# Q and K of both attention layers in two float32r parts, two heads in the row halves of TensorE

## What is computed

```
def attention0(x):                                   # layer 0
    q, k, v = split(x @ Wqkv)                        # 16 heads, 16 dimensions each
    scores = einsum('bhqd,bhkd->bhqk', q, k) * hd ** -0.5
    scores = where(causal, scores, -inf)
    return einsum('bhqk,bhkd->bhqd', softmax(scores), v) @ Wproj + bproj

mod = silu(cond) @ Wada + bada                       # shifts, scales and gates
x = x + gate_a * attention0(norm(x) * (1 + scale_a) + shift_a)
x = x + gate_m * (gelu((norm(x) * (1 + scale_m) + shift_m) @ W1 + b1) @ W2 + b2)

h = gamma * norm(x) + beta                           # layer 1
q, k, v = split(h @ Wqkv1.T + bqkv)
att = softmax(einsum('bhqd,bhkd->bhqk', q, k)) / sqrt(D)
h1 = einsum('bhqk,bhkd->bhqd', att, v) @ Wp.T + bp + x
return gamma * norm(h1) + beta + h1
```

## Time and profile before

| | |
|---|---|
| median of 3 runs | 1240.19 us (1234.33 to 1240.56) |
| profiled execution, its own time | 1239.17 us |
| its span, first to last instruction | 1237.4 us |
| mean granted TensorE clock | 0.986 of full speed |
| PE busy | 1164.9 us (94%) |
| DVE busy | 849.1 us (69%) |
| ACT busy | 676.6 us (55%) |
| POOL busy | 279.7 us (23%) |

### The profile page before, as it was taken

One profiled execution on the slowest core, in us unless ns is written; L12 is line 12 of the kernel. 1 busy time (PEld: TensorE's weight loads), 2 busy tenths in 40 slices (PEclk: granted clock), 3 DMA queues, 4 the chain that ended last, 5 costly groups with the idle time before them and its releaser, 6 DMA issues.

```text
span 1237.4 us, 18599 instructions
## 1 busy us (share of the span) xinstructions
PE 1164.9 (94%) x6604; PEld 591.7 (48%) x6604; DVE 849.1 (69%) x1779; ACT 676.6 (55%) x1346; POOL 279.7 (23%) x378
## 2 busy tenths in 40 slices
PE   7888999999999998999899999999989999999995
PEld 5434644464444644555345644546445553445332
DVE  4835498637886579836887379855888368764775
ACT  1173245656557465565656466565645656553673
POOL 1133032311432024301233013320233002310003
PEclk9799999999999999999999999999999999999999
DMA  4603031302432042500623024410425005200311
GB/s 166 206 2 103 3 124 33 107 14 72 111 93 65 18 113 71 139 2 18 164 44 115 2 80 104 105 54 18 118 66 139 1 2 148 55 17 32 86 33 43
DMA packets 59190, 89.35 MB, mean 72 GB/s; under 512 B 12914, under 2 KB 23762, under 8 KB 59098
## 3 DMA queue, kind: packets, MB, share of 16 engines
q1 hardware_dynamic: 58078, 87.35, 25.4%
q10 hardware_dynamic: 1020, 0.81, 0.2%
HBM read 24.41 MB, written 4.70 MB: 24 GB/s over the span
## 4 chain that ended last, share of the span: by engine, by line
PE 63%; DVE 19%; ACT 5%; SPq 5%; DMA 3%; issue 3%; POOL 1%; ACTq 0%; DVEq 0%; POOLq 0%
PE X L1037 15%; DVE MX L759 10%; PE OP L942 10%; PE X L1064 9%; PE X L1088 9%; PE SC L953 8%; PE X L972 8%; SPq L416 4%; ACT E L621 3%; DMA OC<-OE 2%; DVE STAT L768 2%; DVE XN L808 2%; DVE XR L875 1%; DVE TMP L871 1%; PE X L1052 1%
## 5 line engine op out<-in xcount | busy, mean ns | idle before, releaser
L759 DVE TENSOR_REDUCE MX<-X 128x1 f32<-128x512 f32 (+3 forms) x1024 | 533.2, 583 | 178.4 <-PE X L975 95.4
L621 ACT ACTIVATE E<-SC 128x512 f32<-128x512 f32 (+3 forms) x1024 | 459.0, 524 | 325.8 <-PE SC L953 258.6
L972 PE MATMUL X<-KS,QS 96*128 96x512 bf16 (+3 forms) x1024 | 296.5, 346 | 11.6 <-DVE MX L759 7.5
L953 PE MATMUL SC<-QS,KS 99*128 99x512 bf16 (+3 forms) x1024 | 276.1, 342 | 19.6 <-ACT E L621 12.6
L942 PE MATMUL OP<-E,V 128*32 128x512 f32 (+3 forms) x2048 | 208.2, 524 | 5.2 <-ACT OE L636 5.0
L953 PEld LDWEIGHTS SC<-QS,KS 99*128 99x128 bf16 x1024 | 93.7, 97 | 168.3 <-ACT E L621 105.9
L972 PEld LDWEIGHTS X<-KS,QS 96*128 96x128 bf16 x1024 | 97.4, 98 | 160.2 <-DVE MX L759 52.9
L541 POOL TENSOR_SCALAR_AFFINE_SELECT E<-E 128x512 f32<-128x512 f32 x128 | 87.0, 683 | 249.1 <-ACT E L621 249.1
L1088 PE MATMUL X<-XT,W 128*128 128x512 f32 x256 | 119.1, 598 | 1.2 <-ACT XT L651 1.2
L1064 PE MATMUL X<-XT,WQKV 128*128 128x512 f32 x256 | 118.2, 607 | 1.4 <-ACT XT L651 1.4
L1037 PE MATMUL X<-W,HID 128*128 128x256 f32 x512 | 115.3, 380 | 0.3 <-ACT HID L671 0.3
(11 more groups left out here) (92 smaller groups left out, 922.9 us busy)
## 6 DMA issues: line engine op xcount, KB each, us to landing
QS<-PART SPq DMA_DIRECT2D x192, 128.0 KB, 2.4
KS<-PART SPq DMA_DIRECT2D x192, 128.0 KB, 2.5
OC<-OE SPq DMA_DIRECT2D x56, 128.0 KB, 3.8
RB<-recip_sums SPq DMA_DIRECT2D x56, 128.0 KB, 2.6
XIN<-in_x SPq DMA_DIRECT2D x8, 512.0 KB, 4.9
ROW<-row_vectors SPq DMA_DIRECT2D x8, 512.0 KB, 3.7
out<-OUT SPq DMA_DIRECT2D x7, 512.0 KB, 3.2
W<-in_w SPq DMA_DIRECT2D x2, 1024.0 KB, 7.3
```

Of the source, the lines that this page charges most:

```text
L621: a.activation(E[:, at["tick"].index() % 3, j, lo:T], SC[(at["head"].index() + j) % 3][:, lo:T], ACT.Exp, scale=HD ** -0.5 if layer == 0 e ...
L759: v.reduce_max(MX[:, qt, h:h + 1], X[at["bank"].index() % BANKS][:, 0:w], AX.X, negate=True)\
L953: t_.matmul(SC[(at["head"].index() + j) % 3][:, lo:T], KS[stacks(layer, b)][0:ALL_ROWS, h, kt * P:kt * P + P], QS[stacks(layer, b)][0:ALL_ ...
L972: ins = t_.matmul(bank[:, 0:w], QS[stacks(layer, b)][0:CUT_ROWS, h, qt * P:qt * P + P], KS[stacks(layer, b)][0:CUT_ROWS, h, 0:w], start=Tr ...
```

## The change

- Q and K are cut into two float32r parts instead of three bf16 ones. ACT writes the high part, DVE the low part directly; X32 and the third cut are gone. Three products of parts matter, so a head takes 3 rows for each dimension, 48, and a spare fourth row, 64 in all. The spare rows are zero but for two that hold the maximum in two parts (in QS) and ones (in KS). Scans and scores use the same 64 rows, so the maximum's rows in QS are zeroed by a DMA before each stack.
- Even heads stand on partitions 0 to 63, odd ones on 64 to 127, so that a matmul uses 64 rows of the array (tile size 64 x 128 in the built program, where before it is 128 x 128). Scans of the two heads of a pair alternate, tile by tile.
- The mask has 128 rows and a half has 64, so it takes two matmuls (L995, L996), of 128 and 64 columns.
- SyncE issues 14 DMAs for Q and K of a layer and batch, 256 KB each but two of 64 KB, instead of 24 of 128 KB.
- Spare rows are zeroed at the start by four DMAs of 512 KB; condition tiles move into R1 and constants into RH.
- HEAD, RING and TAIL are written anew; at the start `mods` moves ahead of `turn_a`.

```diff
-CUTS = 6
-CUT_ROWS = CUTS * HD
-ALL_ROWS = CUT_ROWS + 3
-Q_PARTS = (0, 0, 0, 1, 1, 2)
-K_PARTS = (0, 1, 2, 0, 1, 0)
+CUTS = 3
+SPARE = CUTS
+ROWS_PER_DIM = CUTS + 1
+HALF_ROWS = ROWS_PER_DIM * HD
+MAX_ROWS = slice(SPARE, P, 32)
+Q_PARTS = (0, 0, 1)
+K_PARTS = (0, 1, 0)
...
 HEAD = """
-    stat_a norm_a turn_a q0 stackq0 k0 stackk0 mods rows s v0 s s s s s s s s s s s s s s s s s s s s s s s s s
...
+    stat_a norm_a mods turn_a q0 stackq0 k0 stackk0 rows v0 s s s s s s s s s s s s s s s s s s s s nm0_0 s
...
+def scan_tiles(layer):
+    return [(2 * pair + u, qt) for pair in range(PAIRS) for qt in range(TT) for u in range(2)]
+def rows_of(h):
+    return slice(HALF_ROWS * (h % 2), HALF_ROWS * (h % 2) + HALF_ROWS)
...
-            sp.wait_ge(ones_pool, 1)
+            sp.wait_ge(ones_pool, 3)
             for n in range(2):
-                sp.dma_start(KS[n][CUT_ROWS:ALL_ROWS, :, :], ONES).then_inc(ones_load, 16)
+                for stacked in (QS, KS):
+                    sp.dma_start(stacked[n][SPARE:P:ROWS_PER_DIM, :, :], SPARES).then_inc(spare_load[n], 16)
+            for n in range(2):
+                sp.wait_ge(spare_load[n], 32)
+                sp.dma_start(KS[n][MAX_ROWS, :, :], ONES).then_inc(ones_load, 16)
...
-                for part in range(3):
-                    wait(sp, (high_act, cut_low, cut_low)[part], ready[part])
+                if side == 0:
+                    sp.dma_start(QS[n][MAX_ROWS, pairs, :], ZERO[:]).then_inc(stack_dma[n][half], 16)
+                for part in range(2):
+                    wait(sp, (high_act, dense_dve)[part], ready[part] + half)
                     for r in range(CUTS):
                         if parts[r] == part:
-                            sp.dma_start((QS, KS)[side][n][r:CUT_ROWS:CUTS, heads, :],
-                                         PART[rows, side, part, :, :]).then_inc(stack_dma[n][half], 16)
+                            sp.dma_start((QS, KS)[side][n][r:P:ROWS_PER_DIM, pairs, :],
+                                         PART[:, side, part, half, :]).then_inc(stack_dma[n][half], 16)
...
-                        if t == 0:
-                            wait(dve, cut_low, at["low"].at())
                         if what[1] == "0":
-                            ins = v.tensor_tensor(X32[:, t, :], bank(t)[:], part[:, 0, t, :], ALU.subtract)
+                            ins = v.tensor_tensor(low, bank(t)[:], high, ALU.subtract)
...
-                    if what[1] == "1" or b == 0:
-                        wait(dve, dense_dve, at["by_dve"].at(1, 2))
-                        v.tensor_copy(part[:, 1], X32[:]).then_inc(cut_low, 1)
-                        wait(dve, cut_low, at["low"].at(1, 1))
-                        v.tensor_tensor(part[:, 2], X32[:], part[:, 1], ALU.subtract).then_inc(cut_low, 1)
...
-                t_.matmul(SC[(at["head"].index() + j) % 3][:, lo:T], KS[stacks(layer, b)][0:ALL_ROWS, h, kt * P:kt * P + P],
-                          QS[stacks(layer, b)][0:ALL_ROWS, h, lo:T], start=True, stop=True).then_inc(head_full, 1)
+                rows, n = rows_of(h), stacks(layer, b)
+                t_.matmul(SC[(at["head"].index() + j) % 3][:, lo:T], KSR[n][rows, h // 2, kt * P:kt * P + P],
+                          QSR[n][rows, h // 2, lo:T], start=True, stop=True).then_inc(head_full, 1)
...
-                ins = t_.matmul(bank[:, 0:w], QS[stacks(layer, b)][0:CUT_ROWS, h, qt * P:qt * P + P],
-                                KS[stacks(layer, b)][0:CUT_ROWS, h, 0:w], start=True, stop=layer == 1)
+                ins = t_.matmul(bank[:, 0:w], QSR[n][rows, h // 2, qt * P:qt * P + P],
+                                KSR[n][rows, h // 2, 0:w], start=True, stop=layer == 1)
                 if layer == 0:
-                    ins = t_.matmul(bank[:, qt * P:w], ID16[:], CAUSAL[:], start=False, stop=True)
+                    t_.matmul(bank[:, qt * P:w], IDR[rows, HALF_ROWS:3 * HALF_ROWS], CAUSAL[rows, :], start=False, stop=False)
+                    ins = t_.matmul(bank[:, qt * P + HALF_ROWS:w], IDR[rows, 0:P], CAUSAL[rows, 0:HALF_ROWS],
+                                    start=False, stop=True)
```

More of the change, by code:

```diff
@@ L216, in one_list @@
     groups = [(layer, b, s // TT) for layer, b, s in products if s % TT == TT - 1]
-    tiles = [(layer, b, n // TT, n % TT) for i in passes
+    tiles = [(layer, b, *scan_tiles(layer)[n]) for i in passes
              for layer, b, first, end in ((0, i, H * TT // 2 + EARLY, H * TT), (1, i - 1, 0, H * TT),
@@ L657, in work @@
                     for t in range(2):
[L658 removed]
+                        part, psum = PARTR[:, side, 0, t, :], bank(t)
                         if t == 0:
                             for half in range(2):
[L661 to L662 removed]
+                                wait(act, stack_dma[0][half], at["stack0"].at(STACKED))
+                                wait(act, stack_dma[1][half], at["stack1"].at(STACKED))
                         if what[1] == "0":
@@ L678, in work @@
                 elif what.startswith("max"):
-                    n, heads = int(what[3]), maxima_heads(what)
-                    rows = 3 * (heads.stop - heads.start)
+                    n, pairs = int(what[3]), maxima_pairs(what)
+                    rows = 4 * (pairs.stop - pairs.start)
                     psum = bank(0)
@@ L967, in scan @@
                 if h % (H // 2) == 0 and qt == 0:
-                    wait(pe, stack_dma[stacks(layer, b)][h // (H // 2)], 192 * (b + 1 + layer - stacks(layer, b)))
+                    wait(pe, stack_dma[stacks(layer, b)][h // (H // 2)], STACKED * (b + 1 + layer - stacks(layer, b)))
+                    if b == 0 and layer == 0:
+                        pe.wait_ge(spare_load[0], 32)
+                        pe.wait_ge(mask_load, 32)
+                    if b == 0 and layer == 1:
+                        pe.wait_ge(spare_load[1], 32)
                 claim(at["bank"].at(), scan_done, at["scan"].at(1, 1))
@@ L1111, in work @@
                 elif what.startswith("max"):
-                    wait(pe, max_pool, at["maxima"].at(4, 4))
-                    psum = bank(0).bitcast(BF16)
-                    heads = maxima_heads(what)
-                    rows = 3 * (heads.stop - heads.start)
+                    wait(pe, max_pool, at["maxima"].at(2, 2))
+                    psum = bank(0)
+                    pairs = maxima_pairs(what)
+                    rows = 4 * (pairs.stop - pairs.start)
                     for qt in range(TT):
-                        ins = t_.transpose(psum[0:rows, qt * P:qt * P + P], NMP[:, qt, 0:rows], ID16[:])
+                        ins = t_.transpose(psum[0:rows, qt * P:qt * P + P], NMP[:, qt, 0:rows].bitcast(F32), ID32[:])
                     ins.then_inc(dense_full, 1)
```

191 lines of the change are left out of this document (95 added, 96 removed).

## The result

The changed kernel takes 1298.66 us (median of 4 runs, 1295.49 to 1307.12), the kernel before 1239.89 beside it on the same chip. The ratio is 1.0496, with a 95% interval of 1.0445 to 1.0546: 59 us slower, where 49 us faster was forecast. The time lies above the range.

What follows compares the result with a forecast made beforehand. TensorE (PE) was taken as the bound. The profiled span 1237.4 - 76 (stream gain after waits) + 23 (mode changes) + 3 (start) = 1187, with 1.8 around it 1189, and median runs 1.0 higher: 1190 us, range 1115 to 1290.

Steps and rivals of the forecast that it cites:

- I take bf16's rate and full overlap between the halves: Scans and scores: 512-column matmuls at 0.108 us each, touched stream 288 us instead of 390, a change of -102.
- rival 4: Wide float32r matmuls: halves don't overlap (1349 us) or each streams like a float32 record (1375); break-even 0.17 each; chance 0.19.
- the load's 0.11: TensorE weight loads: 4-byte weights of 128 columns take some 0.11 us each, read from the small modulation matmuls.
- rival 2: Weight loads go one after another despite the halves, 0.11 us each: 1226 us, up to 1236; chance 0.13.
- The share of waits: TensorE waiting for banks that DVE and ACT free: a quarter of the 102 us gain lost, leaving -76.
- The sum of 390 us: TensorE's stream that the change touches, before it: scans, scores and masks, 390 of 1237 us.
- Layer 0's tiles: Layer 0's scans with two masks each: 0.28 us a tile, 143 us for 512 against 102 before, losing 41.
- Changes of mode: Switching TensorE's tiling: about 0.1 us each, 259 more changes, 26 us at most, taken as +23, lower end 0.
- Cutting: Dropping the third part of Q and K: 34.6 us less of DVE, counted at 0, lower end -10.
- The start: Modulation matmuls ahead of the first Q and K, and zeros through SyncE's queue: +3 us, ends 0 and +10.
- The signs I had named: Start distances, records per matmul, PE's share below 94%, DVE's near 69%, DVE's waits for PE shrinking, PE's for DVE and ACT growing.
- The last condition: Forecast wrong if time stands above 1234 us with halves overlapping: then the loss is in masks, switches or the order.

Runs made afterwards that it cites:

- new lists: The kernel before with the changed kernel's HEAD, RING and TAIL, nothing else changed: 1245.0 us, ratio 1.0043 to the kernel before.
- bf16 over all rows: The changed kernel with bf16 for stacks, parts, masks and maxima, and every scan, score and mask over all 128 rows: 1229.0 us, ratio 0.9907 to the kernel before.
- bf16 halves: The changed kernel with bf16 instead of float32r for stacks, parts, masks and maxima, row halves kept: 1229.4 us, ratio 0.9912 to the kernel before.

## Why the prediction was wrong

**The ledger.** The 59 us, from kernel to kernel: new lists +5 (1239.9 to 1245.0), lighter cutting, two parts and the second mask together, in bf16 over all rows, -16 (to 1229.0), float32r +97 (to 1325.8), halves -27 (to 1298.7). The last is some -73 of matmuls side by side and +46 of clock. Seen the other way, 44 of the 59 us are the clock's share (60 against 16) and 15 are the rest, where the forecast had -49 and no clock.

**The step that failed** is "I take bf16's rate and full overlap between the halves" for 1152 wide matmuls at 0.108 each. The rate was nearly right (one record, 0.235 us for 512 columns) and the overlap is real, but it is far from full. The table has the touched stream, from start to start in the trace, without the half of the time that it spent at the lower clock, and what the prediction had for the change, all in us:

| part | before | after | change | forecast |
|---|---|---|---|---|
| wide scans and scores, 1280 | 323 | 287 | -36 | -124 |
| narrow scores, 384 | 78 | 76 | -2 | -21 |
| layer 0's narrow scans, all masks | 98 | 127 | +29 | +41 |
| together | 499 | 490 | -9 | -102 |

Three things keep the wide ones from 0.108. First, wide matmuls follow one another 830 times, and only 271 times do two begin within 0.05 us (255 in bf16 halves); if each had a wide partner, it would be at least half of the times. Second, a pair in float32r holds PE for 0.34 us and not 0.22. With 0.17 a pair member, my own break-even of rival 4 (0.17) was reached. In bf16 the pair takes 0.23 (670.10 to 670.33), so the difference is the type's; I had the load's 0.11 in hand and counted it only for masks, and rival 2 named it only as a floor under narrow matmuls. Third, the long stretches: six wide matmuls and a product take 1.61 us where 6 x 0.108 would be 0.65, and in bf16 halves still 1.39; the stretch from 211.08 shows how, with a score that waits for a bank that ACT's exps free. How much of the missing 88 us each of the three costs, no run separates.

**What was missing altogether** is the clock. The sum went by the earlier trace rows at 0.986, and nothing in them is on half the array, so no row could tell; but 44 us more of clock's share is nearly as large as the forecast gain. I should have kept a term for it, since the earlier trace rows show the clock at 0.85 and 0.92 in the two stretches where PE is less busy.

**The other terms.** *The share of waits*: a quarter of the gain was too little. The sum of 390 us is what matmuls need; in the trace they hold PE for 505 us before (what they wait included), 524 after, 491 in bf16 over all rows and 464 in bf16 halves. The rows I read for waits were PE's own; the loads of scores waited for ACT for 105.9 us before already. ACT's exp at 0.53 us is more than twice a score, and there are three banks. *Layer 0's tiles*: 0.28 forecast, and +41 us; the clock included, the narrow scans and masks grew by just that, from 101 to 142, but 12 of it are the clock's, so the agreement is in part luck. Alone, a tile costs the scan + 0.10, then 0.06 and 0.08, so 0.40 for 384 columns; where two lie side by side, both together cost 0.42 (581.22 to 581.64 in after), below my 0.28 each:

```profile
581.22 0.45 PE L992 MATMUL X<-KS,QS 64*128 64x384 f32 x2
581.50 0.23 PE L995 MATMUL X<-CAUSAL,IDR 64*128 64x128 f32 x2
581.56 0.25 PE L996 MATMUL X<-CAUSAL,IDR 64*128 64x64 f32 x2
581.64 0.48 PE L992 MATMUL X<-KS,QS 64*128 64x512 f32 x1
```

*Changes of mode*: 0.1 each is right in bf16; leaving a wide float32r matmul in a half for a dense one costs 0.19 (0.42 against 0.24). Whether +23 was right in sum, no run isolates. *Cutting*: counted at 0; with two parts, the second mask and the use of all 128 rows beside it, it gave -16, 12 of them clock (1245.0 and 0.982 against 1229.0 and 0.992). *The start*: the first scan begins 4.4 us later than in the earlier trace rows, within 0 to +10 and near my +3:

```profile
39.60 0.33 PE L992 MATMUL X<-KS,QS 64*128 64x128 f32 x2
```

**The signs I had named.** Wide scans in different halves near 0 apart, then 0.2: they are at 0 and then 0.34. One record: yes. PE's share below 94%: no, 95%. PE's waits growing: slightly, against the earlier trace rows:

```profile
ACT E L643 <- PE SC L967: 303.0, 165, 13.8
...
PE SC L967 <- ACT E L643: 16.2, 50, 0.6
```

DVE's waits for PE did not shrink but grew. The last condition held, time above 1234 with halves overlapping, but the loss it pointed to (masks, switches or order) was only partly there: masks cost 74 us over all rows and 13 in halves, and the order gained. Rival 4 had the sign and 1349 or 1375, by mechanisms that aren't there as it had them: the halves do overlap, and a record doesn't stream at 0.43.

## What to carry to other kernels

Price a matmul by its stream, its weight load *and* what stands behind it: here the same float32r scan cost 0.02 us more than in bf16 ahead of a wide matmul and 0.10 more ahead of a mask. Before counting on two matmuls side by side, count in the order how many really have a partner next to them. Before making an engine's stream shorter, find what frees the buffers it fills: here the long stretches kept their old length, with scores waiting for ACT's exps of 0.53 us. And when a change makes TensorE work on part of its rows, or gives it less to do, read the granted clock of every variant beside its time: here it took back 23 to 46 us of what the halves gave. Take the clock from the same executions as the time; in after the profiled one had 0.945 and the median 0.954, a difference of 12 us.

## What the runs showed of the hardware

- Matmuls on 64 of 128 rows lower the granted clock, whatever their type: 0.865 and 0.932 when all scans and scores are on one half (float32r, bf16), 0.954 and 0.973 on two halves, against 0.990 and 0.992 on all rows, with the same counts and order of matmuls in all but the second of them. In float32r on one half PE was busy for 98% of the span, and the clock of that execution was still 0.859.
- Less work for TensorE can take more time: masks out of bf16 halves, 1229.4 to 1235.8 us, clock 0.973 to 0.954.
- A float32r matmul is one record and streams nearly at bf16's rate (0.235 against 0.216 us from wide to wide), but a mask behind a wide scan comes 0.10 us later than in bf16 (0.32 against 0.22), and a pair on two halves takes 0.34 against 0.23; 97 us for 3072 matmuls over all rows.
- Two row halves begin within 0.01 us of each other. A change between the whole array and row halves costs 0.09 to 0.1 us each way in bf16, and 0.19 on going from a wide float32r matmul in a half to a dense one.
